# A fused cross-attention and mixture-of-experts kernel: the router's steps at other slots of the round

## The chip, the cores and the metric

The kernel runs on one core of a Trainium2 chip. It is one launch; the metric is the device time of that launch in microseconds. Five engines work side by side, each on its own list of instructions, and meet only at semaphores: TensorE (PE, matrix products and transposes), VectorE (DVE), ScalarE (ACT), GpSimd (POOL) and SyncE (SP, which here issues all the DMAs).

## The reference, cut to what matters

The input x has 64 batches of 256 tokens with 256 features; ctx has 64 x 77 tokens of 256 features. Everything is float32.

```python
# 1: gated cross-attention, 4 heads of 64, RMS norm on q and k
xn = layernorm(x)
q = rms(xn @ Wq); k, v = split(ctx @ Wkv); k = rms(k)
a = softmax(q k^T / 8) v
x1 = x + tanh(g_xattn) * (a @ Wfc + fc_b)
# 2: gated mixture of 8 experts (256 x 256 each), top 2, capacity 97 for each batch
x2 = layernorm(x1)
logits = x2 @ Wr^T                       # 8 for each token
top_vals, top_idx = top_k(logits, 2)
w = softmax(top_vals)
pos = how many earlier choices of the batch took the same expert
keep = pos < 97
out = x1 + tanh(g_ffn) * sum over the 2 choices of keep * w * (x2 @ We[expert])
```

## The kernel before, in words

**Tiling.** The 64 batches are handled in 32 pairs. A pair is 512 tokens, which is 4 tiles (t = 0 to 3) of 128 partitions. Every float32 product of size is made from three float32r products: each operand is split into a high part (a copy rounded to float32r, written by ScalarE) and a low part (the remainder, a subtraction by VectorE), and high x high, high x low and low x high are added in PSUM. Where the kernel says `x2T_part`, `pT_part`, `o_part`, `q` and so on for ScalarE, that is the high copy; the function of the same name for VectorE is the remainder, which waits for that copy.

**The experts.** All 8 experts are computed for all tokens, and a gate per token and expert, which is zero for the experts not chosen or over capacity, scales each result. Product c of a pair (`moe(m, c)`, c = 0 to 15) is tile c // 4 against experts 2*(c % 4) and 2*(c % 4) + 1: six matmuls of 512 columns into bank bkM0 (c even) or bkM1 (c odd). VectorE empties bkM0 (`experts`, c even: two operations that add into acc_v), ScalarE empties bkM1 (`experts`, c odd: two scaled copies into a_out). Product c waits until product c - 2 has been emptied. GpSimd adds the copies (`finish_tile`: three a_sum and one y for a tile).

**The pipeline.** Three pairs are at work in one round: m (its experts), p, one pair later (output projection, second layernorm, router) and f, two pairs later (attention). A round has 16 slots, k = 0 to 15, one for each expert product. On TensorE slot k is `moe(m, k)` and then the listed steps of p and f. ScalarE and VectorE have lists of their own by slot, GpSimd one list (`slots`). These lists, written out by hand, are the order of the instructions on the engine; nothing is reordered later. A loop body holds two rounds and runs 14 times; two rounds fill the pipeline before it, one full round precedes it, and three follow, of which the first still has all three pairs.

**The attention of f in the second half of a round.** TensorE computes scores(t) into four banks. VectorE takes row_max(t): s_max from the bank, then s_bias = -s_max * q_r. ScalarE does exps(t): four activations with a sum for each head. VectorE does inverse(t), GpSimd normalise(t) (L437), TensorE p_transpose(t) back into the bank, ScalarE and VectorE pT_part(t), and TensorE attend(m, b), which for b = 0 needs the parts of tiles 0 and 1 and for b = 1 those of tiles 2 and 3. ScalarE and VectorE then split the result (o_part).

**The router of p.** TensorE transposes xn2 (x2_transpose, two banks); ScalarE and VectorE split it (x2T_part). TensorE makes logits (four matmuls); ScalarE copies them (`logits`), TensorE turns them (logits_transpose, four small transposes, L1172). VectorE's route(p, 0) makes lg_lo, lg, top, eq, rank, first, mask and lg2 for the first choice (L866 to L885); route(p, 1) makes top, gap, eq, rank, first, mask and `both` for the second (L871 to L888; `both` is the only one that writes bf16). ScalarE's router_exp is one small activation of gap. TensorE's positions (L1180 to L1183) counts earlier choices by four small bf16 matmuls on `both`. VectorE's gates makes den, w_top, g_part, g_all and two gate operations (L900 to L915), which scale the experts one round later. The banks of logits, lg_ps and pos_ps are parts of bkC, which is also a bank of attend(1, b); so attend(1, 0) waits for gates.

**Lines.** L305 is the helper of all products, L511 of ScalarE's high copies, L729 of VectorE's remainders, L606 ScalarE's experts, L933 VectorE's experts, L450 and L455 GpSimd's a_sum and y, L416 its xb, L566 exps, L822 and L826 row_max, L1132 p_transpose.

Of the kernel before, what the change touches and what calls it, by code (L numbers as in the profile page):

```python
# [69 lines left out]
def build(nc, x, ctx_in, g_xattn, g_ffn, Wq, Wkv, Wfc, fc_b, qn_w, kn_w, Wr, We, out):  # L70
    es = ExitStack()
    with es:  # L72
# [421 lines left out]
        def _(act):  # L494
# [116 lines left out]
            def slot(k, m, p, f):  # L611
# [23 lines left out]
                if k == 7:  # L635
                    if f:
                        q(f, 0)
                        q(f, 1)
                    if p:
                        x2T_part(p, 0)  # L640
                        x2T_part(p, 1)
                    if m:
                        experts(m, k)
                if k == 8 and f:
                    k_part(f)
                if k == 9:
                    if p:
                        logits(p)
                    if f:
                        exps(f, 0)  # L650
                    if m:
                        experts(m, k)
                    if f:
                        exps(f, 1)
# [5 lines left out]
                if k == 12 and f:  # L660
                    exps(f, 3)
                if k == 13:
                    if f:
                        pT_part(f, 0)
                        pT_part(f, 1)
                    if p:
                        router_exp(p)
                    if m:
                        experts(m, k)
                    if f:  # L670
                        pT_part(f, 2)
                        pT_part(f, 3)
# [25 lines left out]
        def _(dve):  # L698
# [238 lines left out]
            def slot(k, m, p, f):  # L937
# [38 lines left out]
                if k == 7:  # L976
                    if f:
                        q(f, 1)
                    if p:
                        x2T_part(p, 0)  # L980
                        x2T_part(p, 1)
                if k == 8:
                    if f:
                        q_mean(f)
                        k_part(f)
                    if m:
                        experts(m, k)
                if k == 9 and f:
                    row_max(f, 0)
                    row_max(f, 1)  # L990
                    row_max(f, 2)
                    row_max(f, 3)
                if k == 10 and m:
                    experts(m, k)
                if k == 11:
                    if f:
                        inverse(f, 0)
                    if p:
                        route(p, 0)
                    if f:  # L1000
                        inverse(f, 1)
                        inverse(f, 2)
                if k == 12:
# [4 lines left out]
                    if p:  # L1008
                        route(p, 1)
# [3 lines left out]
                if k == 14:  # L1013
                    if f:
                        pT_part(f, 2)
                        pT_part(f, 3)
                    if p:
                        gates(p)
# [24 lines left out]
        def _(pe):  # L1043
# [141 lines left out]
            def slot(k, m, p, f):  # L1185
# [14 lines left out]
                if k == 5 and f:  # L1200
                    q(f, 0)
                if k == 6:
                    if f:
                        q(f, 1)
# [3 lines left out]
                if k == 7 and f:  # L1208
                    q_squares(f)
                    k_transpose(f)  # L1210
                if k == 8:
                    if p:
                        logits(p)
                    if f:
                        scores(f, 0)
                if k == 9 and f:
# [3 lines left out]
                if k == 10 and p:  # L1220
                    logits_transpose(p)
                if k == 13 and f:
                    p_transpose(f, 0)
                    p_transpose(f, 1)
                    p_transpose(f, 2)
                    p_transpose(f, 3)
                if k == 14:
                    if p:
                        positions(p)
                    if f:  # L1230
                        attend(f, 0, 0, p)
# [46 lines left out]
```

## Time and profile before

| | before |
|---|---|
| median of 3 runs | 1496.6 us (1494.82 to 1496.76) |
| span of the profiled execution | 1506.5 us |
| PE busy (matmul) | 1433.3 us, 95% |
| VectorE busy | 1093.6 us, 73% |
| ScalarE busy | 888.2 us, 59% |
| GpSimd busy | 764.2 us, 51% |
| mean DMA rate | 28 GB/s |

The span runs from the first to the last instruction of one profiled execution, so its length and the median of the timed runs are two measurements. A line of a timeline gives start and duration in microseconds from the span's start, the engine, the line of the kernel, the operation, what it writes and reads, and in brackets the idle time ahead of it with what ended it. Matmuls are pipelined: a group's duration includes the last one's way through the array, so the next group starts before it is over.

### The profile page before, as it was taken

The numbers are of one execution on the slowest core, as the hardware profiler recorded it, in microseconds if no ns is written. First come the engines' busy times: TensorE is split into PE (matmuls) and PEld (weight loads), VectorE is DVE, ScalarE is ACT, GpSimd is POOL, SyncE is SP. The second block draws the span as 40 slices with busy tenths as digits, with TensorE's granted clock in tenths as the row PEclk, the third lists the DMA queues.
The fourth block names the chain that finished last, engine by engine and source line by source line (L and its number), as shares of the span: only waits on it lengthen the run. The fifth ranks groups of instructions, "written<-read, shape, count | busy, mean of one in ns | idle before, by whom it ended". The sixth has DMA issues, their size and how long they took to land. (4 is left out here: it accounts for less than half of the span.)

```text
span 1506.5 us, 30216 instructions
## 1 busy us (share of the span) xinstructions
PE 1433.3 (95%) x8320; PEld 1194.0 (79%) x8320; DVE 1093.6 (73%) x3085; ACT 888.2 (59%) x2536; POOL 764.2 (51%) x915
## 2 busy tenths in 40 slices
PE   5899999999999999999999999999999999999998
PEld 4688887878788887887878878787888878878886
DVE  5667767777777677767778777777776777677763
ACT  6546656656566556566556566565566566666552
POOL 3335455445455445555545555444655554554454
PEclk8689999999999999999999999999999999999999
DMA  4000000000000000000000000000000000000000
GB/s 142 19 1 33 33 31 10 32 26 32 33 15 25 33 25 33 32 10 30 25 33 32 33 7 32 26 32 33 32 7 33 25 33 32 22 18 32 8 16 27
DMA packets 29021, 42.76 MB, mean 28 GB/s; under 512 B 4672, under 2 KB 12288, under 8 KB 28928
## 3 DMA queue, kind: packets, MB, share of 16 engines
q1 hardware_dynamic: 28928, 41.90, 8.1%
q14 instruction: 81, 0.66, 0.1%
q8 instruction: 12, 0.20, 0.1%
HBM read 25.11 MB, written 16.78 MB: 28 GB/s over the span
## 5 line engine op out<-in xcount | busy, mean ns | idle before, releaser
L305 PE MATMUL bkM<-we,x2T 128*128 128x512 f32 x3072 | 789.8, 399 | 1.1 <-DVE acc_v L933 1.1
L305 PEld LDWEIGHTS bkM<-we,x2T 128*128 128x128 f32 x3072 | 556.0, 189 | 110.6 <-DVE acc_v L933 1.8
L606 ACT ACTIVATE a_out<-bkM,gate 128x256 f32<-128x256 f32 x512 | 215.2, 475 | 187.4 <-PE bkM L305 185.1
L450 POOL TENSOR_TENSOR a_sum<-a_sum,a_out 128x256 f32<-128x256 f32 x256 | 188.4, 736 | 131.4 <-ACT a_out L606 112.7
L933 DVE SCALAR_TENSOR_TENSOR acc_v<-bkM,gate,acc_v 128x256 f32<-128x256 f32 x384 | 185.6, 483 | 36.8 <-PE bkM L305 27.0
L406 POOL TENSOR_TENSOR rstd<-ve,minus_half 128x4 f32<-128x4 f32 x64 | 64.8, 1012 | 256.6 <-DVE ve L740 256.6
L406 POOL TENSOR_TENSOR q_r<-q_ve,minus_half 128x16 f32<-128x16 f32 x32 | 93.2, 2911 | 135.0 <-DVE q_ve L816 135.0
L517 ACT ACTIVATE xn<-x_sb,shift,rstd 128x256 f32<-128x256 f32 x128 | 66.5, 590 | 111.8 <-DVE shift L749 111.8
L437 POOL TENSOR_TENSOR probs<-probs,p_inv 128x308 f32<-128x308 f32 x128 | 90.3, 716 | 79.1 <-DVE p_inv L831 79.1
L406 POOL TENSOR_TENSOR k_r<-k_ve,minus_half 77x8 f32<-77x8 f32 x32 | 52.3, 1633 | 122.1 <-DVE k_ve L789 122.1
L455 POOL TENSOR_TENSOR y<-a_sum,acc_v 128x256 f32<-128x256 f32 x128 | 94.0, 735 | 10.9
L450 POOL TENSOR_TENSOR a_sum<-a_out 128x256 f32<-128x256 f32 x128 | 93.9, 734 | 3.9 <-ACT a_out L606 3.9
L416 POOL TENSOR_TENSOR xb<-x_sb,bias_g 128x256 f32<-128x256 f32 x128 | 93.8, 744 | 0.0
L305 PE MATMUL bkF<-pT,vz 77*128 77x256 f32 x384 | 60.5, 296 | 31.0 <-DVE pT L729 31.0
L305 PEld LDWEIGHTS bkF<-pT,vz 77*128 77x128 f32 x384 | 54.0, 197 | 35.9 <-issue 33.4
L933 DVE SCALAR_TENSOR_TENSOR acc_v<-bkM,gate,x 128x256 f32<-128x256 f32 x128 | 61.8, 483 | 27.9 <-PE bkM L305 24.2
L566 ACT ACTIVATE probs<-bkA,s_bias,q_r 128x77 f32<-128x77 f32 x128 | 51.4, 413 | 44.6 <-DVE s_bias L826 44.6
L525 ACT ACTIVATE xn<-x,shift,rstd 128x256 f32<-128x256 f32 x128 | 66.2, 592 | 0.6 <-DVE shift L749 0.6
L1114 PEld LDWEIGHTS bkE<-head_ones,q_sq 128*128 128x128 f32 x512 | 61.9, 192 | 3.7 <-issue 1.3
L1114 PE MATMUL bkE<-head_ones,q_sq 128*128 128x2 f32 x512 | 59.1, 246 | 0.9 <-DVE kn L795 0.9
L305 PEld LDWEIGHTS bkA<-wfc,oT 128*128 128x128 f32 x384 | 50.1, 193 | 9.3 <-DVE oT L729 7.8
L305 PE MATMUL bkD<-wkv,cT 128*77 128x512 f32 x192 | 51.1, 402 | 5.8 <-DVE wkv L720 5.8
(162 smaller groups left out, 2799.1 us busy)
## 6 DMA issues: line engine op xcount, KB each, us to landing
x_sb<-in_x SPq DMA_DIRECT2D x32, 512.0 KB, 3.6
out<-y SPq DMA_DIRECT2D x64, 256.0 KB, 2.0
ctx_sb<-in_ctx SPq DMA_DIRECT2D x32, 154.0 KB
stage<-in_L_ffn_We SPq DMA_DIRECT2D x2, 1024.0 KB, 8.0
stage<-in_L_xattn_Wkv SPq DMA_DIRECT2D x1, 512.0 KB, 5.9
stage<-in_L_xattn_Wq SPq DMA_DIRECT2D x1, 256.0 KB, 6.2
stage<-in_L_xattn_Wfc SPq DMA_DIRECT2D x1, 256.0 KB, 4.1
bias_bc<-in_L_xattn_fc_b SPq DMA_DIRECT2D x1, 128.0 KB, 5.3
```

What stands on the lines that cost most here:

```text
L305: mm = nc.tensor.matmul(out, l, r, start=(i == 0), stop=(i == len(terms) - 1))
L406: return nc.gpsimd.tensor_tensor(dst, src, minus_half[0:parts, 0:n], ALU.pow)
L416: nc.gpsimd.tensor_tensor(xb[:, t], x_sb[:, f.parity, t], bias_g[:], ALU.add).then_inc(xb_done.sem, 1)
L437: nc.gpsimd.tensor_tensor(pr, pr, p_inv[:, t].unsqueeze(2).to_broadcast([P, H, LK]), ALU.mult).then_inc(probs_done.sem, 1)
L450: nc.gpsimd.tensor_tensor(a, o[:, 0] if i == 1 else a, o[:, i], ALU.add).then_inc(a_summed.sem, 1)
L455: nc.gpsimd.tensor_tensor(y[:, t], a, acc_v[:, t], ALU.add).then_inc(y_done[t].sem, 1)
L517: nc.scalar.activation(xn1[:, t], x_sb[:, f.parity, t], ACT.Identity, scale=rstd1[:, t:t + 1], bias=shift1[:, t:t + 1]).then_inc(xn1_done. ...
L525: nc.scalar.activation(xn2[:, t], x1[:, p.parity, t], ACT.Identity, scale=rstd2[:, t:t + 1], bias=shift2[:, t:t + 1]).then_inc(xn2_done.se ...
L566: ins = nc.scalar.activation(probs[:, t, h * LK:(h + 1) * LK], s_bank[t][:, h * LK:(h + 1) * LK], ACT.Exp, scale=q_r[:, t, h:h + 1], bias= ...
L606: ins = nc.scalar.activation(a_out[:, t % 2, (e // 4) * 2 + i], bkM[1][:, i * D:(i + 1) * D], ACT.Copy, scale=gate[:, m.parity, t, e:e + 1])
L933: nc.vector.scalar_tensor_tensor(out=acc_v[:, t], in0=bkM[0][:, i * D:(i + 1) * D], scalar=gate[:, m.parity, t, e:e + 1], in1=src, op0=ALU ...
L1114: mm = pe.matmul(ssq_ps[:, c0:c0 + 2], q_sq[:, m, t * P:(t + 1) * P], head_ones[:], start=True, stop=True)
```

## The change

The router's steps stand at other slots. On TensorE the two x2 transposes go from slot 6 (behind q(1)) to slot 5 (behind q(0)), the logits from slot 8 to slot 7, their transposes from slot 10 to slot 8, and the positions from slot 14 to slot 13, ahead of the p transposes. On ScalarE the x2T copies go ahead of q(1) in slot 7, the copy of the logits from slot 9 to 8, router_exp from slot 13 to 12. On VectorE the x2T remainders go ahead of q(1) in slot 7 (q(1) itself from the front of the slot to its end), route(0) from slot 11 to slot 9, between row_max(0) and row_max(1), with inverse(0) behind row_max(2); row_max(3) and inverse(1) go to slot 10 behind the experts; route(1) from slot 12 to slot 11; gates in slot 14 from behind the pT remainders of tiles 2 and 3 to ahead of them. No instruction is added or taken away.

```diff
--- before.py
+++ after.py
@@ -635,17 +635,19 @@
                 if k == 7:
                     if f:
                         q(f, 0)
-                        q(f, 1)
                     if p:
                         x2T_part(p, 0)
                         x2T_part(p, 1)
-                    if m:
-                        experts(m, k)
-                if k == 8 and f:
-                    k_part(f)
+                    if f:
+                        q(f, 1)
+                    if m:
+                        experts(m, k)
+                if k == 8:
+                    if f:
+                        k_part(f)
+                    if p:
+                        logits(p)
                 if k == 9:
-                    if p:
-                        logits(p)
                     if f:
                         exps(f, 0)
                     if m:
@@ -657,14 +659,15 @@
                         exps(f, 2)
                     if m:
                         experts(m, k)
-                if k == 12 and f:
-                    exps(f, 3)
+                if k == 12:
+                    if f:
+                        exps(f, 3)
+                    if p:
+                        router_exp(p)
                 if k == 13:
                     if f:
                         pT_part(f, 0)
                         pT_part(f, 1)
-                    if p:
-                        router_exp(p)
                     if m:
                         experts(m, k)
                     if f:
@@ -974,48 +977,51 @@
                     if m:
                         experts(m, k)
                 if k == 7:
-                    if f:
-                        q(f, 1)
                     if p:
                         x2T_part(p, 0)
                         x2T_part(p, 1)
+                    if f:
+                        q(f, 1)
                 if k == 8:
                     if f:
                         q_mean(f)
                         k_part(f)
                     if m:
                         experts(m, k)
-                if k == 9 and f:
-                    row_max(f, 0)
-                    row_max(f, 1)
-                    row_max(f, 2)
-                    row_max(f, 3)
-                if k == 10 and m:
-                    experts(m, k)
+                if k == 9:
+                    if f:
+                        row_max(f, 0)
+                    if p:
+                        route(p, 0)
+                    if f:
+                        row_max(f, 1)
+                        row_max(f, 2)
+                        inverse(f, 0)
+                if k == 10:
+                    if m:
+                        experts(m, k)
+                    if f:
+                        row_max(f, 3)
+                        inverse(f, 1)
                 if k == 11:
-                    if f:
-                        inverse(f, 0)
-                    if p:
-                        route(p, 0)
-                    if f:
-                        inverse(f, 1)
+                    if p:
+                        route(p, 1)
+                    if f:
                         inverse(f, 2)
                 if k == 12:
                     if m:
                         experts(m, k)
                     if f:
                         inverse(f, 3)
-                    if p:
-                        route(p, 1)
                 if k == 13 and f:
                     pT_part(f, 0)
                     pT_part(f, 1)
                 if k == 14:
+                    if p:
+                        gates(p)
                     if f:
                         pT_part(f, 2)
                         pT_part(f, 3)
-                    if p:
-                        gates(p)
                     if m:
                         experts(m, k)
                     if f:
@@ -1197,38 +1203,39 @@
                 if k == 3 and f:
                     x_transpose(f)
                     kv(f, 1)
-                if k == 5 and f:
-                    q(f, 0)
-                if k == 6:
-                    if f:
-                        q(f, 1)
+                if k == 5:
+                    if f:
+                        q(f, 0)
                     if p:
                         x2_transpose(p, 0)
                         x2_transpose(p, 1)
-                if k == 7 and f:
-                    q_squares(f)
-                    k_transpose(f)
+                if k == 6 and f:
+                    q(f, 1)
+                if k == 7:
+                    if f:
+                        q_squares(f)
+                        k_transpose(f)
+                    if p:
+                        logits(p)
                 if k == 8:
-                    if p:
-                        logits(p)
                     if f:
                         scores(f, 0)
+                    if p:
+                        logits_transpose(p)
                 if k == 9 and f:
                     scores(f, 1)
                     scores(f, 2)
                     scores(f, 3)
-                if k == 10 and p:
-                    logits_transpose(p)
-                if k == 13 and f:
-                    p_transpose(f, 0)
-                    p_transpose(f, 1)
-                    p_transpose(f, 2)
-                    p_transpose(f, 3)
-                if k == 14:
+                if k == 13:
                     if p:
                         positions(p)
                     if f:
-                        attend(f, 0, 0, p)
+                        p_transpose(f, 0)
+                        p_transpose(f, 1)
+                        p_transpose(f, 2)
+                        p_transpose(f, 3)
+                if k == 14 and f:
+                    attend(f, 0, 0, p)
                 if k == 15 and f:
                     attend(f, 0, 1, p)
                     attend(f, 1, 0, p)
```

## Rows read from the trace of the kernel before

**Rows 1.** The page of the profiled execution, its first part: busy time of each engine.

```profile
PE 1433.3 (95%) x8320; PEld 1194.0 (79%) x8320; DVE 1093.6 (73%) x3085; ACT 888.2 (59%) x2536; POOL 764.2 (51%) x915
```

**Rows 2.** TensorE's waits over the whole span: total us, times, longest.

```profile
PE bkF L305 <- DVE pT L729: 31.0, 32, 1.0
```

**Rows 3.** Two adjoining rounds, busy time; then granted clock, DMA share, GB/s.

```profile
721.27:766.21 44.94, 43.85 (x263) 36.83 (x262) 34.14 (x97) 27.57 (x79) 23.74 (x29) 1.00 0.08 27
766.21:812.40 46.19, 44.26 (x263) 36.63 (x262) 33.69 (x97) 27.32 (x79) 23.71 (x29) 1.00 0.08 27
```

**Rows 4.** Timeline of TensorE: start, duration, operation, count, idle before it.

```profile
746.26 1.10 PE L1164 MATMUL bkC<-x2T,wr 128*16 128x512 f32 x4
...
752.74 0.42 PE L1172 MATMUL bkC<-ident,lgT 16*128 16x16 f32 x4
753.09 4.40 PE L305 MATMUL bkM<-we,x2T 128*128 128x512 f32 x18
757.33 0.60 PE L1132 MATMUL bkA<-ident,probs 128*77 128x128 f32 x4
...
758.99 1.63 PE L305 MATMUL bkM<-we,x2T 128*128 128x512 f32 x6
760.68 0.18 PE L1180 MATMUL bkC<-both,before 128*128 128x16 bf16 x1
...
761.97 0.94 PE L305 MATMUL bkF<-pT,vz 77*128 77x256 f32 x6 [1.03 <-DVE pT L729]
...
764.13 0.87 PE L305 MATMUL bkF<-pT,vz 77*128 77x256 f32 x6
```

**Rows 5.** Timeline of VectorE, the same round and columns.

```profile
748.54 0.75 DVE L826 SCALAR_TENSOR_TENSOR s_bias<-s_max,q_r 128x4 f32<-128x4 f32 x1
...
753.96 0.16 DVE L866 COPY lg_lo<-bkC 128x32 f32<-128x32 f32 x1
...
755.58 0.19 DVE L885 SCALAR_TENSOR_TENSOR lg<-mask,lg 128x32 f32<-128x32 f32 x1
...
757.38 0.19 DVE L871 TENSOR_REDUCE top<-lg 128x4 f32<-128x32 f32 x1
...
759.25 0.56 DVE L882 TENSOR_TENSOR mask<-rank,first 128x32 f32<-128x32 f32 x1
759.85 0.78 DVE L888 TENSOR_TENSOR both<-mask 128x32 bf16<-128x32 f32 x1
...
761.15 0.67 DVE L729 TENSOR_TENSOR pT<-bkB,pT 77x512 fp32r<-77x512 f32 x1
...
762.94 0.15 DVE L900 TENSOR_SCALAR den<-egap 128x4 f32<-128x4 f32 x1
...
764.03 0.26 DVE L915 SCALAR_TENSOR_TENSOR gate<-bkC,g_all 128x16 f32<-128x16 f32 x2
```

**Rows 6.** Timeline of ScalarE, the same round.

```profile
749.33 0.42 ACT L566 ACTIVATE probs<-bkA,s_bias,q_r 128x77 f32<-128x77 f32 x1 [1.34 <-DVE s_bias L826]
...
751.62 0.44 ACT L566 ACTIVATE probs<-bkB,s_bias,q_r 128x77 f32<-128x77 f32 x1
...
754.78 0.87 ACT L606 ACTIVATE a_out<-bkM,gate 128x256 f32<-128x256 f32 x2
...
757.97 0.59 ACT L511 ACTIVATE pT<-bkA 77x512 fp32r<-77x512 f32 x1 [0.72 <-PE bkA L1132]
```

**Rows 7.** Timeline of GpSimd, the same round.

```profile
749.23 0.73 POOL L450 TENSOR_TENSOR a_sum<-a_out 128x256 f32<-128x256 f32 x1
750.03 1.54 POOL L450 TENSOR_TENSOR a_sum<-a_sum,a_out 128x256 f32<-128x256 f32 x2
751.65 0.74 POOL L455 TENSOR_TENSOR y<-a_sum,acc_v 128x256 f32<-128x256 f32 x1
752.35 0.73 POOL L416 TENSOR_TENSOR xb<-x_sb,bias_g 128x256 f32<-128x256 f32 x1
...
759.02 1.55 POOL L450 TENSOR_TENSOR a_sum<-a_sum,a_out 128x256 f32<-128x256 f32 x2
```

More of the change, by code:

```diff
@@ L641, in slot @@
                         x2T_part(p, 1)
+                    if f:
+                        q(f, 1)
                     if m:
                         experts(m, k)
-                if k == 8 and f:
-                    k_part(f)
-                if k == 9:
+                if k == 8:
+                    if f:
+                        k_part(f)
                     if p:
                         logits(p)
+                if k == 9:
                     if f:
@@ L987, in slot @@
                         experts(m, k)
-                if k == 9 and f:
-                    row_max(f, 0)
-                    row_max(f, 1)
-                    row_max(f, 2)
-                    row_max(f, 3)
-                if k == 10 and m:
-                    experts(m, k)
-                if k == 11:
+                if k == 9:
                     if f:
-                        inverse(f, 0)
+                        row_max(f, 0)
                     if p:
@@ L1000, in slot @@
                     if f:
+                        row_max(f, 1)
[6 more added lines that the diff above has]
+                        row_max(f, 3)
                         inverse(f, 1)
+                if k == 11:
+                    if p:
+                        route(p, 1)
+                    if f:
                         inverse(f, 2)
@@ L1207, in slot @@
                         x2_transpose(p, 1)
-                if k == 7 and f:
-                    q_squares(f)
-                    k_transpose(f)
-                if k == 8:
+                if k == 6 and f:
[4 more added lines that the diff above has]
+                        k_transpose(f)
                     if p:
                         logits(p)
+                if k == 8:
                     if f:
                         scores(f, 0)
+                    if p:
+                        logits_transpose(p)
                 if k == 9 and f:
```

## The prediction

> **What bounds the kernel now.** I read the page's busy line first: TensorE is busy 95% of the span, VectorE 73%, ScalarE 59%, GpSimd 51% [rows 1]. So the time is TensorE's list, plus what it waits. Next, who TensorE waits for: one line recurs once a pair, the attention product into bkF behind VectorE's pT, 32 times and at most 1.0 us [rows 2]. Two adjoining rounds at full granted clock take 44.94 and 46.19 us [rows 3]; the second contains the loop's jump. I then laid the four engines' timelines of the first of these rounds side by side from its ninth slot on [rows 4 to 7]; all times below are of this round. In them the reader is to see three things.
>
> First, the real size of the stall. Eighteen expert matmuls (three products) advance TensorE from 753.09 to 757.33, 1.41 us a product. The product of slot 14 starts at 758.99, so TensorE is free at 760.40, but attend(0,0) starts at 761.97. Between lie only the four small positions matmuls, some 0.1 us. About 1.45 us is lost: positions waits for `both`, which ends at 760.63, and attend for the second pT remainder, which ends at 761.82 [rows 4, 5]. ScalarE had the high parts of pT ready from 758.56 on [rows 6], so VectorE was late, because route(1) filled it until 760.63.
>
> Second, why route is long. Route(0) went from 753.96 to 755.77, 1.8 us for nine operations. Route(1), eight like them, took 3.2 us. `both` takes 0.78 us where a like operation takes 0.19, and it ends at 760.63 as a GpSimd a_sum ends at 760.57; s_bias starts at 748.54 and takes 0.75 us, to 749.29 [rows 5, 7]. So a VectorE operation with two SBUF operands that starts while GpSimd is at work ends only 0.02 to 0.06 us after that GpSimd instruction. The s_max, pT and expert operations, which read PSUM, are not stretched.
>
> The Trainium skill says of this (SBUF — State Buffer, Who interferes with whom) that the two engines share a port pair as an exclusive lock, and whoever is second is blocked for the whole instruction. By that rule, the trace agrees: 0.78 against 0.19 us. Without it one would sum the unblocked lengths and come to rival 2 below, a gain.
>
> Third, two tight places. ScalarE runs exps(0), experts(9), exps(1), exps(2), experts(11), exps(3) without a pause from 749.33; experts(11) ends at 755.65 and TensorE's product 13, which overwrites that bank, comes at 755.91 (753.09 + 2 x 1.41). That is 0.26 us of slack [rows 4, 6].
>
> **The change part by part.** No instruction is added or removed and no DMA is moved; SP's queue and GpSimd's keep their order. What changes is who stands behind whom.
>
> *x2 transposes to slot 5, x2T before q(1), logits to slot 7.* TensorE's sum is the same. xn2 and the x2T halves are ready with more than 1 us to spare, as ScalarE and VectorE wait in that stretch today. Cost 0, bounds -0.3 to +0.3 us a round (the copies it passes take 0.6 us). Product 8 now stands behind the logits (about 1 us [rows 4]), so VectorE does experts(8) at 747.4 to 748.4. s_max(0) still ends before 748.9, and s_bias(0) ends at 749.29 as today, held by GpSimd. Cost 0.
>
> *Logits transposes to slot 8.* 0.35 us (752.74 to 753.09) stands two products earlier. ScalarE's copy of the logits ends near 746.7, the transposes come at 747.8: no wait.
>
> *route(0) between row_max(0) and row_max(1).* This is the costly edit. Waiting behind it on VectorE are s_bias(1), and through it exps(1), exps(2), experts(11) and exps(3) on ScalarE. Route(0) starts at 749.26 and meets GpSimd's chain of 749.23 to 753.08 [rows 7]. By today's steps (0.19, 0.23, 0.22 us apart) eq starts at 749.90, where the GpSimd instruction is nearly over, and ends at 750.09. rank starts at 750.12, in the next a_sum, and ends at 750.8; mask, in the third, at 751.6. lg2 starts at about 751.66, where y starts at 751.65: the pair mask and `both` stood in just this phase (759.85 against an a_sum that starts near 759.83), and `both` was held [rows 5, 7]. So lg2 ends at 752.43. s_max(1) follows to 752.9, and s_bias(1) is held by xb until 753.11. exps(1) starts at 753.15 instead of 751.62: 1.53 us late. The bounds are 0 (nothing held) and 2.2 us (eq held as well); I take 1.53.
>
> *What is late next.* From 753.15, by today's lengths (exps 1.58 us each, experts 0.87 to the end), exps(2) starts at 754.72, experts(11) at 756.31, and ends at 757.18. Product 13 starts at 757.22 instead of 755.91: 1.3 us of TensorE. About 0.4 of it is also spent at product 12, which waits for experts(10) until about 754.9; these overlap and aren't added.
>
> *route(1) to slot 11, positions ahead of the p transposes.* route(1) ends near 757.5, before TensorE asks at 758.64. Positions cost 0.15 us there. Transposes follow at 758.79 (757.33 today), product 14 at 760.45. The last softmax quarter is ready at 759.6, before its transposes at 760.1. The two pT remainders end at 760.7 and 761.3, and attend(0,0) runs at 761.86, without a wait. The stall of 1.45 us is gone, but 1.3 us was spent before: a gain of 0.1 at this point.
>
> *gates ahead of pT(2) and pT(3).* Here attend(0,1), which asks at 764.0 (0.78 + 1.38 us later, as today), waits for more. Gates last 1.35 us today (762.94 to 764.29) with GpSimd idle. Now they start at 761.27 while GpSimd is at a_sum until 761.94 and at y until 762.75 (its list stands behind the last softmax quarter, which is ready at 759.6; from there 1.55 us for two a_sum and 0.74 for y [rows 7]). w_top(1) is held to 761.98, the two g_part slip through behind it, g_all is held by y to 762.8, the gates end at 763.1, pT(3) at 764.4, and attend(0,1) starts at 764.54 instead of 764.13. Bounds of gates: 1.35 us (unheld) and 3.0 us (held four times). I take 1.85, by the nearest row, the two held operations of route(1).
>
> **Sum.** +0.41 us at attend(0,1). What follows it (the rest of attend, the jump, the oT chain) hangs on it and keeps its distance. There are 30 rounds with all three pairs at work: 30 x 0.41 = 12.3 us. The round that fills has no experts, so its softmax chain is open to route(0)'s delay; the one that drains loses a short wait for `both`: together +1, bounds -2 to +3. Sum +13 us. The profiled execution goes from a span of 1506.5 to about 1520. Its span is 9.9 us above the median of the runs shown, before what lies around it; the change acts on the rounds, which repeat, so I add the difference to the median: 1496.6 + 13 = 1509.6.
>
> **Rivals.**
> 1. *lg2 slips in ahead of y.* It turns on a hundredth of a microsecond. s_bias(1) ends at 752.46, exps(1) is 0.88 us late, product 13 0.66, attend(0,0) comes at 761.2 and attend(0,1) at 763.85: -0.28 us a round, -8 us, 1488. For it: of 32 `both` the shortest is 0.19 us, so some slip through. Against it: their median is 0.778 us, and the phase is the same each round. Chance 0.17.
> 2. *The cover holds*: route(0) is short, exps(1) isn't delayed, and the removed stall is nearly all kept. It decides if exps(1) starts before 751.9. Then attend(0,1) comes some 1.2 us earlier, -36 us, 1461. For it: 1.8 us of route(0) would end at 751.05. Against: two-operand operations at this very place are held today. Chance 0.13.
> 3. *den is held too.* den is a one-operand operation; if those are also held by GpSimd, it goes to 761.98, w_top(1) to 762.8, g_all to 763.6, pT(3) to 765.2, attend(0,1) to 765.35: +1.2 a round, +36 us, 1533. No row shows such an operation under a GpSimd instruction, either way. The Trainium skill names tensor_scalar among those that can take both ports (SBUF — State Buffer, Who interferes with whom); no run here shows it. Chance 0.12.
> 4. *It cancels*, a round within 0.1 us of today's: 1497. The change then does in effect nothing: the wait goes from bkF to product 13 and no more. Chance 0.10.
>
> **How the numbers follow.** Forecast 0.48, with its own range 1502 to 1520. Slower by over 0.2% (3 us, about what a measurement of this kernel can tell) are the forecast and rival 3: 0.60. Faster are 1 and 2: 0.30. Same: 0.10. The range 1482 to 1530 holds the forecast, 1, 4 and the near part of 3, and leaves out rival 2 and the far part of 3.
>
> **What would show it.** Right: TensorE's wait at bkF behind pT for attend(0,0) is gone; in its place stand waits of the product into bkM for ScalarE's a_out and, before attend(0,1), for pT; ScalarE waits 1.4 us for s_bias(1) before exps(1); lg2, 0.19 us in all 32 of today, has a median near 0.75; rounds take 45.3 and 46.6 us. Wrong: rounds of 43.7 (rival 2), lg2 at 0.19 us (rival 1), den over 0.5 us (rival 3), or a wait at the logits, which I cost at nothing.

## The result and the profile after

The changed kernel takes 1539.3 us (median of 4, 1527.9 to 1546.0) against 1496.3 us (median of 4, 1494.8 to 1496.8): ratio 1.028, 95% interval 1.0238 to 1.0322. It is slower, as forecast, but by 43 us instead of the forecast 13, and outside the range.

The page's busy lines of the changed kernel answer to [rows 1]. No instruction is added, yet TensorE is busy 18.8 us longer, in a span that is 32.8 us longer than the 1506.5 of before. (The medians are 43.1 us apart. The other 10 us come from the kernel before, whose profiled execution took longer than its timed ones; more on this under before_again.)

```profile
span 1539.3 us, 30216 instructions
...
PE 1452.1 (94%) x8320; PEld 1200.7 (78%) x8320; DVE 1101.4 (72%) x3085; ACT 894.9 (58%) x2536; POOL 767.2 (50%) x915
```

Next, TensorE's waits (total, times, longest), the answer to [rows 2].

```profile
PE bkF L305 <- DVE pT L732: 33.8, 32, 1.5
PE bkM L305 <- ACT a_out L606: 13.2, 28, 0.5
```

The wait for `pT` stands where it stood by its name, but it is another one: ahead of attend(0,1), not attend(0,0). The wait for a_out is new. Both were forecast. Four rounds of the changed kernel, in the columns of [rows 3]:

```profile
271.30:316.12 44.82, 43.98 (x262) 36.67 (x261) 33.01 (x96) 27.80 (x79) 23.86 (x28) 1.00 0.08 27
547.46:594.83 47.37, 45.61 (x262) 37.89 (x261) 34.40 (x97) 27.79 (x79) 23.81 (x28) 0.96 0.09 30
735.61:781.42 45.81, 44.04 (x261) 36.72 (x260) 33.92 (x96) 27.79 (x79) 23.82 (x28) 1.00 0.08 27
781.42:829.69 48.27, 44.75 (x262) 36.47 (x260) 34.86 (x97) 27.54 (x79) 23.82 (x28) 1.00 0.07 26
```

The kernel before has two lengths of round, with and without the loop's jump. Here the first three, all without the jump, differ by 2.5 us, and one has a granted clock of 0.96, which no full round of the kernel before between 131 and 1405 us has. The timeline of TensorE in the third of them, to hold against [rows 4]:

```profile
764.61 4.43 PE L305 MATMUL bkM<-we,x2T 128*128 128x512 f32 x18
769.52 1.66 PE L305 MATMUL bkM<-we,x2T 128*128 128x512 f32 x6 [0.47 <-ACT a_out L606]
771.02 0.18 PE L1186 MATMUL bkC<-both,before 128*128 128x16 bf16 x1
...
774.31 0.86 PE L305 MATMUL bkF<-pT,vz 77*128 77x256 f32 x6
775.01 1.54 PE L305 MATMUL bkM<-we,x2T 128*128 128x512 f32 x6
777.85 0.94 PE L305 MATMUL bkF<-pT,vz 77*128 77x256 f32 x6 [1.30 <-DVE pT L732]
```

Products 10 to 12 are over at 768.85 (4.24 us later, as before); product 13 starts at 769.52, so 0.67 us is lost, not 1.3. attend(0,0) at 774.31 waits for nothing. attend(0,1) could start at 776.39 and starts at 777.85: 1.46 us lost. VectorE in that round, for [rows 5]:

```profile
763.14 0.63 DVE L881 TENSOR_TENSOR rank<-eq,first_weight 128x32 f32<-128x32 f32 x1
...
764.61 0.19 DVE L888 SCALAR_TENSOR_TENSOR lg<-mask,lg 128x32 f32<-128x32 f32 x1
...
773.64 0.74 DVE L903 TENSOR_SCALAR den<-egap 128x4 f32<-128x4 f32 x1
774.42 0.18 DVE L905 RECIPROCAL w_top<-den 128x4 f32<-128x4 f32 x1
774.63 0.56 DVE L907 TENSOR_TENSOR w_top<-w_top,egap 128x4 f32<-128x4 f32 x1
...
775.23 0.72 DVE L910 TENSOR_TENSOR g_part<-mask,w_top 128x32 f32<-128x32 f32 x1
...
776.26 0.26 DVE L918 SCALAR_TENSOR_TENSOR gate<-bkC,g_all 128x16 f32<-128x16 f32 x2
```

GpSimd and ScalarE beside them, for [rows 7] and [rows 6]:

```profile
772.81 1.56 POOL L450 TENSOR_TENSOR a_sum<-a_sum,a_out 128x256 f32<-128x256 f32 x2
774.44 0.73 POOL L455 TENSOR_TENSOR y<-a_sum,acc_v 128x256 f32<-128x256 f32 x1
...
762.27 0.42 ACT L566 ACTIVATE probs<-bkA,s_bias,q_r 128x77 f32<-128x77 f32 x1 [2.62 <-DVE s_bias L829]
...
765.45 0.42 ACT L566 ACTIVATE probs<-bkB,s_bias,q_r 128x77 f32<-128x77 f32 x1 [0.76 <-DVE s_bias L829]
```

den ends at 774.38, an a_sum at 774.37; w_top(1) ends at 775.19, y at 775.17. The operations of gates in the short round (271.30 to 316.12):

```profile
309.33 0.16 DVE L903 TENSOR_SCALAR den<-egap 128x4 f32<-128x4 f32 x1
...
309.73 0.38 DVE L907 TENSOR_TENSOR w_top<-w_top,egap 128x4 f32<-128x4 f32 x1
...
310.14 0.19 DVE L910 TENSOR_TENSOR g_part<-mask,w_top 128x32 f32<-128x32 f32 x1
310.37 0.61 DVE L912 TENSOR_TENSOR g_all<-g_part 128x32 f32<-128x32 f32 x1
311.01 0.26 DVE L918 SCALAR_TENSOR_TENSOR gate<-bkC,g_all 128x16 f32<-128x16 f32 x2
```

den is held in the one (0.74 us) and not in the other (0.16). Gates take 2.88 us against 1.94, and TensorE's idle time on the bkF line is 1.30 against 0.37. den was held in 22 of the 29 full rounds. lg2 was not held (0.19 in all rounds), so exps(1) starts 3.18 us behind exps(0), where it was 2.29: route(0) delays it by 0.89 us, and ScalarE waits 0.76 us for s_bias(1), not 1.4.

Counted from the logits of one pair to those of the next, a round without the jump and at full clock lasts 45.8 us where den was held and 44.8 to 44.9 where it was not, against 44.9 before. So there is no round of the 45.3 us forecast; the mean waits come near the forecast, but as a mix of +0.9 and -0.1.

The third cost shows in windows of 2 us behind the long wait of the round at 0.96 (span, PE busy, granted clock, DMA share, GB/s):

```profile
587.50:589.50 2.00, 0.90 (x4) 1.00 0.00 0
589.50:591.50 2.00, 1.81 (x15) 0.97 0.00 0
591.50:593.50 2.00, 2.00 (x8) 0.50 0.33 123
593.50:595.50 2.00, 2.00 (x10) 0.67 0.51 136
595.50:597.50 2.00, 2.00 (x15) 1.00 0.59 218
```

and in the matmuls there:

```profile
589.69 0.94 PE L305 MATMUL bkF<-pT,vz 77*128 77x256 f32 x6 [1.29 <-DVE pT L732]
590.47 2.01 PE L305 MATMUL bkC<-pT,vz 77*128 77x256 f32 x12
592.28 2.71 PE L305 MATMUL bkM<-we,x2T 128*128 128x512 f32 x6
```

TensorE waited from 588.25 to 589.69, worked, and 1.7 us later was granted 1.2 instead of 2.4 GHz for some 3 us; an expert product took 2.71 instead of 1.54 us. Taken over all 2 us windows from 90 to 1440 us with a clock below 0.95, (1 - clock) x 2 us adds up to 16.9 us; in the kernel before there is no such window. That is ten stretches at half clock, all behind a wait of 1.3 us on the bkF line. Of the 32.8 us between the two spans, then, at most 16.9 are the clock and at least 15.9 the waits, 0.53 us a round. At most, because a later wait can take a part back. In the four rounds without the jump the fall costs 1.5 us (47.3 to 47.4 against 45.8). In the six with the jump (47.3 to 48.2) nothing is seen of it: five others with den held and no fall last 47.2 to 48.3, as TensorE waits 0.95 us or more for xn there, and 0.6 or less behind a fall.

### The profile page after: what moved, and what is told of

Same layout as the page of the kernel before. It is cut to its first block and busy times, and to the rows that moved or that the text cites. A ratio compares the mean times of both kernels' runs of the same rounds, so it can differ in the third digit from the quotient of the medians.

```text
span 1539.3 us, 30216 instructions
## 1 busy us (share of the span) xinstructions
PE 1452.1 (94%) x8320; PEld 1200.7 (78%) x8320; DVE 1101.4 (72%) x3085; ACT 894.9 (58%) x2536; POOL 767.2 (50%) x915
## 5 line engine op out<-in xcount | busy, mean ns | idle before, releaser
L305 PE MATMUL bkM<-we,x2T 128*128 128x512 f32 x3072 | 804.5, 404 | 13.9 <-ACT a_out L606 13.2
L305 PEld LDWEIGHTS bkM<-we,x2T 128*128 128x128 f32 x3072 | 564.0, 192 | 148.8 <-ACT a_out L606 25.9
L566 ACT ACTIVATE probs<-bkB,s_bias,q_r 128x77 f32<-128x77 f32 x128 | 51.4, 412 | 21.9 <-DVE s_bias L829 21.8
```

The lines of the kernel that those rows point to most:

```text
L305: mm = nc.tensor.matmul(out, l, r, start=(i == 0), stop=(i == len(terms) - 1))
L566: ins = nc.scalar.activation(probs[:, t, h * LK:(h + 1) * LK], s_bank[t][:, h * LK:(h + 1) * LK], ACT.Exp, scale=q_r[:, t, h:h + 1], bias= ...
```

## Experiments

All totals are medians of timed runs, with the ratio to the kernel before on the same chip.

| kernel | us | ratio, 95% interval |
|---|---|---|
| gates_last | 1490.5 | 0.9987 (0.9978 to 0.9997) |
| route0_later | 1524.3 | 1.0207 (1.0190 to 1.0224) |
| both_undone | 1498.0 | 1.0039 (1.0024 to 1.0053) |
| pool_waits_gates | 1483.3 | 0.9935 (0.9918 to 0.9951) |
| early_only | 1497.5 | 0.9948 (0.9934 to 0.9961) |
| early_and_route0 | 1534.2 | 1.0190 (1.0174 to 1.0207) |
| den_on_scalar | 1503.8 | 0.9989 (0.9975 to 1.0003) |
| pool_waits_both | 1474.4 | 0.9791 (0.9776 to 0.9806) |
| changed_again | 1526.5 | 1.0217 (1.0169 to 1.0265) |
| split_wait | 1529.2 | 1.0242 (1.0224 to 1.0260) |
| pool_waits_route0 | 1503.1 | 1.0076 (1.0060 to 1.0093) |
| gates_last_pool_waits | 1480.9 | 0.9932 (0.9915 to 0.9948) |
| one_long_wait | 1560.7 | 1.0447 (1.0410 to 1.0483) |
| two_waits | 1578.2 | 1.0584 (1.0563 to 1.0604) |
| two_shorter_waits | 1535.2 | 1.0286 (1.0257 to 1.0314) |
| before_again | 1491.5 | 0.9999 (0.9989 to 1.0009) |

The kernel before stood at 1492.1, 1505.6, 1491.4 and 1491.8 us in the four groups (rows 1 to 4, 5 to 8, 9 to 12, 13 to 16); before_again explains this below. It makes the ratios of the second group about 0.9% too low where they are held against the others: against the 1491.4 us of the third group they would be 1.0041 (early_only), 1.0287 (early_and_route0), 1.0083 (den_on_scalar) and 0.9886 (pool_waits_both). Below, versions are therefore compared by their times.

### The two places on VectorE

**gates_last**

```diff
                 if k == 14:
-                    if p:
-                        gates(p)
                     if f:
                         pT_part(f, 2)
                         pT_part(f, 3)
+                    if p:
+                        gates(p)
```

> The changed kernel with one edit undone: gates stands behind the pT remainders of tiles 2 and 3 again. Theory A (the gates, held by GpSimd, delay pT(3) and with it attend(0,1)): the wait ahead of attend(0,1), 1.3 us on the bkF line in most rounds, goes; the wait of product 13 for ScalarE (0.47 us on its line) stays; rounds near 44.3 and 45.6 us, the granted clock stays at 1.00, total 1470 to 1485. Theory B (the router's first part between row_max(0) and row_max(1) is the main cost): total stays above 1515.

**route0_later**

```diff
                         row_max(f, 0)
-                    if p:
-                        route(p, 0)
-                    if f:
                         row_max(f, 1)
                         row_max(f, 2)
+                    if p:
+                        route(p, 0)
+                    if f:
                         inverse(f, 0)
```

> The changed kernel with route(0) behind row_max(2) instead of between row_max(0) and row_max(1). Theory A: product 13 no longer waits for ScalarE (0.67 us of TensorE back), but product 12 may wait up to 0.6 us for experts(10), and the wait ahead of attend(0,1) stays or grows; total 1515 to 1540. Theory B: total falls to about 1500 or below.

**both_undone** is the two together.

> Both edits together: route(0) behind row_max(2) and gates behind the pT remainders of tiles 2 and 3. Theory A: no wait of more than 0.5 us is left in the second half of the round, rounds of 43.7 to 44.2 and 45.0 to 45.5 us, total 1455 to 1475, below gates_last by 0 to 15 us. Theory B: the same total within 5 us as route0_later.

Measured: gates_last takes 36 us less than changed_again. The wait at attend(0,1) is gone and the clock has no low window. Two of its rounds:

```profile
537.11:582.15 45.04, 44.11 (x262) 36.85 (x261) 33.35 (x96) 27.68 (x79) 23.73 (x28) 1.00 0.08 27
989.97:1034.41 44.44, 43.97 (x261) 36.86 (x260) 32.90 (x96) 27.68 (x79) 23.79 (x28) 1.00 0.08 28
```

In the first lg2 takes 0.78 us and product 13 waits 0.77 us on its line; in the second 0.19 and 0.47. The same program goes from one to the other and back in mid-run. This is the hundredth of a microsecond of which the forecast spoke, and the trace shows it: lg2 takes 0.19 us where it starts 1 to 2 ns behind GpSimd's y, and 0.78 where it starts 6 to 8 ns behind; in the changed kernel it is 1 to 2 ns in every full round. At 1490.5 gates_last misses the 1470 to 1485 expected. route0_later is slow still, 2 us below changed_again (product 12 waits 0.52 us for experts(10), as expected; attend(0,1) waits 0.65, less than before and not more), so the gates' place costs most; theory B falls. both_undone misses its expectation by 23 us, and its total is above gates_last: with route(0) behind row_max(2) the wait only goes from product 13 to product 12.

### Is it GpSimd that holds VectorE?

**pool_waits_gates**, **pool_waits_route0** and **pool_waits_both** leave the changed order as it is and keep GpSimd out of the way:

```diff
                 if m:
+                    if p:
+                        pool.wait_ge(top2.sem, top2.at(p, ROUTE_HALF))   # route0, both
                     finish_tile(m, 1)
...
                 if m:
+                    if p:
+                        pool.wait_ge(gate_chain.sem, gate_chain.at(p))   # gates, both
                     finish_tile(m, 2)
```

> The changed kernel with its gates ahead of pT(2) as they are, but GpSimd waits for the gates before it begins finish_tile(2), so nothing of it runs beside them. Theory A (GpSimd's instructions hold the gates' operations): den falls from 0.74 to 0.16 us in all rounds, g_part and g_all to 0.19, the wait ahead of attend(0,1) falls from 1.3 us to 0.4 or less, the clock drops go, total 1485 to 1510. Rival (the 1.35 us of gates themselves, or their place, cost the time and not GpSimd): the wait ahead of attend(0,1) changes by less than 0.3 us and the total by less than 8 us.

> The changed kernel, in which GpSimd waits for route(0) before finish_tile(1) and does not wait for gates. Theory A: product 13 does not wait (route(0) unheld), the wait ahead of attend(0,1) stays at 0.4 or 1.3 us, by whether den is held; total 1490 to 1520. For the clock: if rounds with den held still fall to 0.96, the wait of product 13 is not needed for the fall; if none falls, it is.

> pool_waits_gates, and GpSimd also waits for route(0) before it begins finish_tile(1). Theory A (route(0) is long because GpSimd holds its two-operand operations): route(0) takes 1.8 us instead of 2.4, exps(1) starts at most 0.3 us later than in the kernel before, product 13 does not wait, rounds of 43.6 and 44.6, total 1460 to 1470, below both kernels. Rival (route(0)'s place costs even unheld, or GpSimd becomes late for the softmax): total within 5 us of pool_waits_gates or above it.

pool_waits_gates: den takes 0.16 us in all rounds, the wait ahead of attend(0,1) is gone, and the total is 1483.3, just below the range expected: theory A. pool_waits_route0: product 13 does not wait, but attend(0,1) waits 0.65 us, neither of the two lengths expected, as den is now held for 0.40 to 0.45 us. Its clock does not fall. Since the last wait is half as long there, this does not tell whether the wait of product 13 is needed for a fall; one_long_wait below does.

The waits make a square over the two held chains: 1526.5 us with neither, 1503.1 with route(0) free, 1483.3 with gates free, 1474.4 with both. Freeing route(0) is worth 23 us in the changed kernel and 9 once gates is free; freeing gates 43 and 29. Each wait *added* to GpSimd makes the kernel faster. In pool_waits_both the operations of route(0) are all at 0.19 us,

```profile
558.57 0.19 DVE L885 TENSOR_TENSOR rank<-eq,first_weight 128x32 f32<-128x32 f32 x1
...
559.01 0.19 DVE L889 TENSOR_TENSOR mask<-rank,first 128x32 f32<-128x32 f32 x1
559.24 0.19 DVE L892 SCALAR_TENSOR_TENSOR lg<-mask,lg 128x32 f32<-128x32 f32 x1
```

and TensorE's rounds have no wait left but the one for xn behind the jump:

```profile
531.03:574.98 43.95, 43.93 (x262) 36.73 (x261) 32.33 (x96) 27.69 (x79) 23.79 (x28) 1.00 0.08 28
574.98:619.69 44.71, 44.32 (x262) 36.56 (x260) 33.14 (x97) 27.44 (x79) 23.80 (x28) 1.00 0.08 28
```

It is the fastest version found, 1474 us, below either level of the kernel before. Its total is 4 us above the range expected.

**den_on_scalar** computes den on ScalarE (a Copy with bias 1.0 behind egap), so that gates begins with w_top(0):

```diff
+                act.wait_ge(egap_done.sem, egap_done.at(p))
+                nc.scalar.activation(den[:], egap[:], ACT.Copy, bias=1.0).then_inc(den_done.sem, 1)
...
-                dve.wait_ge(egap_done.sem, egap_done.at(p))
-                did(nc.vector.tensor_scalar(den[:], egap[:], 1.0, None, ALU.add))
-                dve.wait_ge(gate_chain.sem, gate_chain.at(p, 1))
+                dve.wait_ge(den_done.sem, den_done.at(p))
```

> The changed kernel with den computed by ScalarE right behind egap; gates on VectorE begin with w_top(0). Theory A (den, one operand, is held by GpSimd in most rounds and shifts the rest by one GpSimd instruction): all rounds look like the short ones of the changed kernel, wait ahead of attend(0,1) 0.4 us or less, no low clock, total 1500 to 1515. Rival (w_top(1) is held anyway until the same GpSimd instruction ends): wait ahead of attend(0,1) stays 1.0 us or more, total above 1525.

1503.8 us, no fall of the clock, and the wait ahead of attend(0,1) was 0.43 to 0.45 us in every full round: theory A, though w_top(1) and g_all are held (0.54 and 0.61 us). So the one-operand den decides between the short round and the long one. In the two traces of the changed kernel it starts 7 to 16 ns behind an a_sum where it takes 0.16 us, and 15 to 40 ns behind where it takes 0.72 to 0.75. That tensor_scalar can take both ports, when its operands allow it, is what the Trainium skill states (SBUF — State Buffer, Who interferes with whom). By that rule, the trace agrees: 0.74 against 0.16 us. The reciprocals, also of one operand, were never stretched: 0.18 us in all 177 of the kept traces that started well inside a GpSimd instruction.

**gates_last_pool_waits** has gates last and the wait for route(0).

> gates behind the pT remainders of tiles 2 and 3, and GpSimd waits for route(0) before finish_tile(1). Theory A: neither of the two waits is left, rounds of 43.8 to 44.0 and 44.6 to 45.2, total 1465 to 1478, as the best kernel so far within 5 us. Rival: the gates, now late, delay the experts of slot 14 and the total is over 1480.

1480.9 us, rounds of 44.1 and 45.1 without a wait at product 13 or attend: 6.6 us above pool_waits_both, past the 5 us and the 1478 expected, and just over the 1480 of its rival. Of the rival's mechanism little shows: over the whole span the products wait 0.9 us for VectorE's experts.

### The parts that were costed at nothing

**early_only** is the kernel before with the new slots of x2 transposes, x2T and logits alone; **early_and_route0** has also route(0) between row_max(0) and row_max(1).

```diff
                 if k == 9 and f:
                     row_max(f, 0)
+                    if p:
+                        route(p, 0)      # early_and_route0
                     row_max(f, 1)
```

> The kernel before with only the early part of the change: x2 transposes in slot 5, x2T ahead of q(1), logits in slot 7, their copy and transposes in slot 8; route, positions, router_exp and gates stay. The forecast's claim: this costs nothing, rounds of 44.9 and 46.2 us as before, total within 3 us of the kernel before. Rival: the reordering itself costs or gains over 3 us (a wait at the logits or at q(1)).

> early_only, and route(0) between row_max(0) and row_max(1); route(1), positions and gates as before. Theory A (route(0) delays exps(1) by 0.9 to 1.5 us and so product 13 by 0.67 to 1.3): a wait of product 13 for ScalarE appears while the wait of 1.03 us ahead of attend(0,0) stays, since route(1) is not earlier; rounds near 45.6 and 46.9, total 1508 to 1535; by the clock theory (two waits close together, of which one is near 1.5 us, lower the granted clock) rounds with a clock under 0.98 show up as in the changed kernel. Rival: no wait at product 13, or no clock below 0.99.

early_only was 8 us under its neighbour, more than the 3 us expected, and no wait at the logits or at q(1) appears. The kernel before itself stood at 1490 or at 1504 to 1508 us in that group, and early_only (1494 to 1499) lies between, so its cost is not told from nothing. Its rounds:

```profile
535.45:579.89 44.44, 43.63 (x261) 36.89 (x260) 33.08 (x96) 27.62 (x79) 23.76 (x29) 1.00 0.08 28
579.89:625.69 45.80, 44.14 (x262) 36.72 (x261) 33.78 (x97) 27.36 (x79) 23.75 (x29) 1.00 0.07 27
```

early_and_route0 came to 1534, of the size expected, but by another way. VectorE is late for the experts of slot 10, so that product 12 waits 0.22 or 0.75 us, and in the rounds with the jump lg2 is held, product 13 waits 0.15, and attend(0,0) 1.03. Its clock never fell: that part of the expectation was wrong, and its rival (no clock below 0.99) right.

**before_again**

> The kernel before. Its runs have stood at two levels, 1490 to 1494 and 1504 to 1508 us. Expected: by the level of this execution, rounds of 44.9 with gap at 0.66 us (upper level) or of 44.3 to 44.5 with gap at 0.16 us (lower level: one held operation fewer in route(1)), as early_only shows. Rival: the two levels differ in something else (start, clock).

It ran at the lower level, with rounds of 44.34 and 45.61:

```profile
535.88:580.22 44.34, 43.66 (x262) 36.77 (x260) 32.97 (x96) 27.61 (x79) 23.80 (x29) 1.00 0.08 28
580.22:625.83 45.61, 44.13 (x261) 36.60 (x260) 33.66 (x97) 27.36 (x79) 23.79 (x29) 1.00 0.08 27
```

gap is at 0.66 us as in the upper level, so the expected cause is wrong; it is `both` (first and last start, duration from shortest over median to longest, in ns):

```profile
L888 DVE TENSOR_TENSOR both<-mask x32: 191/193/603, 77.3 to 1460.1; 128x32 bf16<-128x32 f32 x32
```

against a median of 778 ns in the trace of [rows 5]. One operation held in 28 rounds or in none, 0.59 us each time, goes with rounds that differ by just under 0.6 us, and that is the 15 us between the spans 1506.5 and 1491.4. In the trace of the upper level `both` starts 7 to 10 ns behind an a_sum in these rounds, in that of the lower level 1 to 5 ns: the same program, decided by less than a hundredth of a microsecond in the phase of two engines. The timed runs beside the changed kernel, 1494.8 to 1496.8 us, are at neither level, and what they held is not known.

### What lowers the clock

**changed_again** is the changed kernel. **split_wait** puts small matmuls into the wait:

```diff
                 if m == 0:
+                    if p and b == 1:
+                        pe.wait_ge(pT_lo.sem, pT_lo.at(f, 3))
+                        pe.wait_ge(gate_chain.sem, gate_chain.at(p))
+                        for _ in range(4):
+                            pe.matmul(pos_ps[:, 0:BP * E], before[:], upto[:, 0:BP * E], start=True, stop=True)
```

**one_long_wait** is gates_last_pool_waits, and **two_waits** and **two_shorter_waits** are gates_last, with

```diff
+                    if now and b == 1:
+                        pe.wait_ge(v_added.sem, v_added.at(now, 16))     # 15 in two_shorter_waits
```

where `now` is the pair m.

> The changed kernel itself, beside the other kernels of this group. It is to show rounds of two lengths (44.8 where den takes 0.16 us, 45.8 where it takes 0.74) and, in about a third of the rounds, a granted clock of 0.96 to 0.97; total 1520 to 1550.

> The changed kernel, with four small matmuls on constants (like those of positions, some 0.1 us) that TensorE issues in the middle of its wait ahead of attend(0,1), once gates is done and tile 2's remainder is there. Nothing is released earlier. Theory C (the granted clock falls behind the long wait that nothing interrupts, as the kernel before waits as long in all at attend(0,0) but with the positions matmuls inside and never falls): den is still held in most rounds, but no round has a clock under 0.98; the total is 8 to 18 us below changed_again. Rival D (it is the sum of the waits of the stretch that counts, or chance): rounds at 0.96 to 0.97 are as frequent as before and the total is within 5 us of changed_again.

> gates_last_pool_waits (no wait of TensorE in the second half of the round, no fall of the clock), in which TensorE waits at attend(0,1) for the end of VectorE's experts of slot 14, some 1.6 us, uninterrupted. Theory C (such a wait alone is enough): rounds with a granted clock of 0.96 to 0.97 appear in a third or more. Rival D (a wait at product 13 ahead of it is needed): the clock is 1.00 in all rounds and each is only longer by 1.5 to 1.7 us; total about 1530.

> gates_last (a wait of 0.7 to 1.0 us at product 13, clock never down) with the same added wait at attend(0,1). Both theories: low rounds appear. If they appear here and not in one_long_wait, the pair of waits is the cause; if in both about as often, the long one. Total 1535 to 1570.

> As two_waits, but TensorE waits at attend(0,1) only for the first of the two operations, some 0.5 us less (about 1.1 us). If the length of the last wait decides, no low round; if the sum of the two does, low rounds as in two_waits but fewer. Total 1510 to 1530.

Per kernel, TensorE's idle time ahead of its line in most rounds; in the profiled execution, from 100 to 1440 us (to 1500 for the last three), the stretches at half clock and the loss over the 2 us windows below 0.95, as above; and the mean granted clock of each of its runs, start and end of the program included:

| kernel | at product 12 or 13 | at attend | stretches | clock loss, us | mean clock of the runs |
|---|---|---|---|---|---|
| before | none | 1.03, positions inside | 0 | 0 | 0.983 to 0.986 |
| pool_waits_route0 | none | 0.65 | 0 | 0 | 0.984 to 0.985 |
| gates_last | 0.5 to 0.8 | none | 0 | 0 | 0.984 to 0.985 |
| changed, changed_again | 0.47 | 1.29 | 10, 8 | 16.9, 13.6 | 0.973 to 0.983 |
| split_wait | 0.5 to 0.8 | 0.78 + 0.16, split | 4 | 6.8 | 0.977 to 0.982 |
| one_long_wait | none | 1.5 | 17 | 32.1 | 0.963 to 0.964 |
| two_waits | 0.5 | 1.6 | 20 | 42.3 | 0.956 to 0.958 |
| two_shorter_waits | 0.5 to 0.8 | 1.1 | 4 | 6.8 | 0.976 to 0.982 |

One long wait is enough, without any at product 13: rival D falls. two_waits has falls about as often, as its expectation said for the case that the long wait is the cause. two_shorter_waits still has four: a last wait of 1.1 us does not rule a fall out with one of 0.5 to 0.8 us ahead of it, though early_and_route0, with 0.75 and 1.03 us, has none. The totals of both are above the ranges expected (1578.2 and 1535.2 us). changed_again did as expected. From gates_last_pool_waits to one_long_wait are 80 us. Rounds without the jump take 44.0 us in the one and in the other 45.6 without a fall and 47.2 to 47.7 with one: 1.7 us for the wait and 1.6 or more for the fall. So of the 80 us, too, the clock is 32 at most. One of the rounds with a fall:

```profile
556.89:604.21 47.32, 45.78 (x261) 37.91 (x260) 33.31 (x97) 27.82 (x79) 23.74 (x28) 0.96 0.09 30
```

In its profiled execution split_wait lost half as much clock as changed_again, but lg2 was held in 18 of its rounds, and the expected 8 to 18 us did not come. Over all runs the mean clocks of the two overlap (table). That splitting a wait saves the clock is not shown. Nor do the runs show why one round in three falls and not each. The falls go with the scatter of the changed kernel's time: the four runs of changed_again took 1540.7, 1532.8, 1520.2 and 1518.3 us at mean clocks of 0.975, 0.978, 0.980 and 0.983.

## Why the forecast was wrong

The forecast was 1509.6 us, the measured median 1539.3, 29.7 above it. At most 16.9 us of that are the clock, about 10 the base, and the remaining 3 the waits, 15.9 where 13 were forecast.

- *The direction and the places* were right: the wait at attend(0,0) went, waits at product 13 and ahead of attend(0,1) came, and their sum was at least +0.53 us a round against the 0.41 forecast. That these two are so near is luck, by the next two points.
- *Product 13, 1.3 us:* 0.67. The step that failed is lg2, taken as held; it slipped in, as in rival 1 (exps(1) 0.89 us late, where the rival had 0.88). The forecast had it start 0.01 us behind y; it started 0.001 to 0.002 behind. Rows read to a hundredth of a microsecond can't decide this.
- *Gates, 1.85 us:* 2.88 in 22 of 29 rounds. The step that failed is den, taken as free, on rows with GpSimd idle; den_on_scalar and pool_waits_gates show it to be rival 3's mechanism. The forecast had both rivals, at 0.17 and 0.12, and treated them as exclusive; both came, and in the sum they nearly cancel.
- *"What follows it ... hangs on it and keeps its distance":* this step has the largest part in the miss. Behind the wait of 1.46 us the granted clock fell in a third of the rounds, and TensorE's own work is stretched by 16.9 us in all. The forecast has no term for the clock. No row of the kernel before shows a clock below full in a full round; its wait of 1.45 us is of the same length in sum but in two pieces. That the break between them is what kept the clock up is not shown (split_wait).
- *"so I add the difference to the median":* the second step that put the time out of range, since 1539.3 less 16.9 is 1522.4, still above 1520. The rows are from an execution of 1506.5 us with `both` held, the median from others near 1496. `both` is never held in the changed kernel, so the change ends a wait that the timed runs of before had, it seems, only in part. The spans differ by 32.8 us, the medians by 43.1. What the timed runs held is not seen in any trace, so this stays argued.
- *The early part, 0:* not told from 0. *Positions ahead of the p transposes:* no wait for `both` in full rounds, as forecast.

## What to carry to other kernels

Where VectorE and GpSimd both work from SBUF, a chain of small two-operand operations is priced by where it falls in GpSimd's list, here up to 0.6 us more for each link (0.78 against 0.19); keep such chains out of GpSimd's busy stretches, or let GpSimd wait for them: two such waits on the engine with room took the kernel from 1526.5 to 1474.4 us here. And a wait of TensorE is to be priced with its clock: in one_long_wait a wait of 1.5 us made a round 1.7 us longer, and over 3 us longer where the clock fell behind it. Last, look at how far the profiled execution lies from the timed runs before its rows are used as their base.

## What the runs showed that was not expected

- One program at two levels, 1491 and 1506 us, with a single operation at 0.19 or 0.78 us.
- A program that changes its phase in mid-run (gates_last, rounds of 45.04 and 44.44 us).
- A one-operand tensor_scalar of four elements held for 0.58 us by GpSimd, while a reciprocal of the same size is not.
- The granted clock at half for about 3 us, beginning 1.6 to 2.1 us after TensorE had gone back to work (changed kernel).
- A fall of the clock that costs 1.5 us in a round without the jump, and nothing visible in one with it, where TensorE would have waited anyway.
